# Moving the product of wide waves and growth from VectorE to GpSimd while a long kernel is made, and one semaphore for two groups of loads

## The reference, cut to what matters

```
dt = exp(log_dt); A = A_re + 1j*A_im; C = C_re + 1j*C_im
dtA = dt[:, None] * A
dC  = C * (exp(dtA) - 1.0) / A
powers = exp(dtA[:, :, None] * arange(L))          # L = 512
K = 2.0 * einsum('dn,dnl->dl', dC, powers).real    # 256 channels, 64 states
```

## Time and profile before

| | |
|---|---|
| median of 3 runs | 1396.36 us (1394.72 to 1397.79) |
| the profiled execution | 1397.99 us, of which its span is 1396.2 us |
| PE | 1192.2 us busy (85% of the span) |
| DVE | 928.4 us (66%) |
| ACT | 476.3 us (34%) |
| POOL | 343.1 us (25%) |
| granted TensorE clock, mean | 0.929 of full speed |

### The profile page before, as it was taken

One profiled execution on the slowest core, in us unless ns is written; L12 is line 12 of the kernel. 1 busy time (PEld: TensorE's weight loads), 2 busy tenths in 40 slices (PEclk: granted clock), 3 DMA queues, 4 the chain that ended last, 5 costly groups with the idle time before them and its releaser, 6 DMA issues. The chain is left out here.

```text
span 1396.2 us, 17324 instructions
## 1 busy us (share of the span) xinstructions
PE 1192.2 (85%) x5149; PEld 694.9 (50%) x5149; DVE 928.4 (66%) x3415; ACT 476.3 (34%) x824; POOL 343.1 (25%) x603
## 2 busy tenths in 40 slices
PE   4666858999899799899989979999687539999997
PEld 3423433455456354545546535554363426667664
DVE  6668898778768777877877787888974581111110
ACT  3543531053324415225332531432414423322221
POOL 4225220023022203302322220330203222323332
PEclk9688978999899999999999999999897759999999
DMA  9102000200300300030030031021000135433321
GB/s 285 36 16 62 19 1 25 52 19 16 92 19 1 100 26 1 16 93 19 6 103 19 1 72 51 1 62 39 1 0 0 63 111 175 137 94 91 95 39 19
DMA packets 45351, 72.51 MB, mean 52 GB/s; under 512 B 8549, under 2 KB 27208, under 8 KB 45130
## 3 DMA queue, kind: packets, MB, share of 16 engines
q1 hardware_dynamic: 39114, 62.88, 15.4%
q0 software_dynamic: 6144, 8.52, 3.5%
HBM read 58.27 MB, written 13.07 MB: 51 GB/s over the span
## 5 line engine op out<-in xcount | busy, mean ns | idle before, releaser
L849 POOL TENSOR_SCALAR ve<-mv 128x2 f32<-128x2 f32 x74 | 17.1, 230 | 501.5 <-DVE mv L1120 501.4
L1703 PE MATMUL ps<-x,keys 128*128 128x512 f32 x256 | 128.3, 627 | 0.9 <-DVE hT L1214 0.6
L1878 PE MATMUL ps<-hT,values 128*128 128x512 f32 x256 | 119.8, 594 | 0.0
L2334 PE MATMUL experts_ps<-experts_yT,experts_fc 128*128 128x512 f32 x256 | 111.9, 595 | 1.2 <-ACT experts_yT L2259 1.2
L2346 PE MATMUL experts_ps<-experts_fc,experts_hT 128*128 128x256 f32 x512 | 112.0, 379 | 0.8 <-ACT experts_hT L2271 0.8
L1703 PE MATMUL ps<-zT_second,w 128*128 128x512 f32 x224 | 104.5, 600 | 6.3 <-ACT big L1641 6.2
L2346 PEld LDWEIGHTS experts_ps<-experts_fc,experts_hT 128*128 128x128 f32 x512 | 96.6, 190 | 14.6 <-ACT experts_hT L2271 1.6
L2243 DVE SCALAR_TENSOR_TENSOR experts_o<-experts_ps,experts_wh,experts_b2w 128x256 f32<-128x256 f32 x32 | 15.5, 484 | 128.6 <-PE experts_ps L2346 128.6
L1703 PE MATMUL ps<-w,big 128*128 128x256 f32 x448 | 99.1, 380 | 0.8 <-ACT big L1641 0.8
L2271 ACT ACTIVATE experts_hT<-experts_ps,experts_b 128x512 f32<-128x512 f32 x64 | 44.0, 687 | 155.3 <-PE experts_ps L2334 155.3
L1703 PEld LDWEIGHTS ps<-w,big 128*128 128x128 f32 x448 | 84.1, 190 | 13.3 <-ACT big L1641 1.6
(11 more groups left out here) (445 smaller groups left out, 2369.4 us busy)
## 6 DMA issues: line engine op xcount, KB each, us to landing
gT<-expert_gates SPq DMA_DIRECT2D x32, 512.0 KB, 7.6
experts_fc<-in_fc1T SPq DMA_DIRECT2D x8, 1024.0 KB, 5.3
experts_fc<-in_fc2T SPq DMA_DIRECT2D x8, 1024.0 KB, 9.1
xT<-in_xT SPq DMA_DIRECT2D x8, 512.0 KB, 3.5
x<-in_x SPq DMA_DIRECT2D x8, 512.0 KB, 3.5
expert_table<-tb SPq DMA_DIRECT2D x7, 528.0 KB, 6.5
out_x<-x SPq DMA_DIRECT2D x7, 512.0 KB, 5.7
w<-in_W SPq DMA_DIRECT2D x2, 1024.0 KB, 9.3
```

The costliest lines, as they stand in the source:

```text
L849: nc.gpsimd.tensor_scalar(o, i, c, None, ALU.add).then_inc(*tick(*event))
L1703: last = nc.tensor.matmul(o, l, r_, start=start, stop=stop)
L1878: last = nc.tensor.matmul(bank("O2", k), S["values"][:, c, k * P:(k + 1) * P], hT[:, c % RING, :], start=(c == 0), stop=(c == HC - 1))
L2334: last = nc.tensor.matmul(g_bank(m), fc1[e % 3][:, k, m * P:(m + 1) * P], yT[e % 2][:, k, :], start=(k == 0), stop=(k == DC - 1))
```

## The change

POOL gets a stage `powers`: it waits for the pass's sines and exponentials and does the wide product, in place, with a signal of its own, `k_lift`. DVE's `powers` loses that product. PE's `powers` waits for both `k_pow` and `k_lift`, and POOL's `phases` from pass 2 on for `k_lift` of pass p-2 as well. As POOL now has a function named `powers`, SCHEDULE puts it, for each pass, where DVE's stands. The three small loads signal `w1_in`, and whoever waited for `w1_in` at 80 or for `row_in` at 48 now waits for `w1_in` at 128.

```diff
+    y.declare("waves_lifted", [("k_lift", p) for p in passes])
...
-            sp.dma_start(S["mgate"][:], A["mod_gate"].partition_broadcast(P)).then_inc(row_in, 16)
-            sp.dma_start(film_row_f[:, 0:2 * D], A["b_film_in"]).then_inc(row_in, 16)
-            sp.dma_start(film_row_f[:, 2 * D:4 * D], A["b_film_out"]).then_inc(row_in, 16)
+            sp.dma_start(S["mgate"][:], A["mod_gate"].partition_broadcast(P)).then_inc(w1_in, 16)
+            sp.dma_start(film_row_f[:, 0:2 * D], A["b_film_in"]).then_inc(w1_in, 16)
+            sp.dma_start(film_row_f[:, 2 * D:4 * D], A["b_film_out"]).then_inc(w1_in, 16)
...
                 if p >= 2:
                     g.wait_ge(*at(0, "k_pow", p - 2))
+                    g.wait_ge(*at(0, "k_lift", p - 2))
...
+            def powers(_, p):
+                k = p % 2
+                g.wait_ge(*at(0, "k_sin", p))
+                g.wait_ge(*at(0, "k_exp", p))
+                g.tensor_tensor(Us[k], Us[k], UEs[k], ALU.mult).then_inc(*tick("k_lift", p))
...
                 v.wait_ge(*at(0, "k_exp", p))
-                nc.vector.tensor_tensor(Us[k], Us[k], UEs[k], ALU.mult)
                 nc.vector.tensor_tensor(WAs[k], WAs[k], WEs[k], ALU.mult).then_inc(*tick("k_pow", p))
...
             def powers(_, p):
                 each = PC // QUARTERS
                 pe.wait_ge(*at(0, "k_pow", p))
+                pe.wait_ge(*at(0, "k_lift", p))
...
-                v.wait_ge(w1_in, 80)
+                v.wait_ge(w1_in, 128)
...
-                v.wait_ge(row_in, 48)
+                v.wait_ge(w1_in, 128)
...
-                        a.wait_ge(row_in, 48)
+                        a.wait_ge(w1_in, 128)
...
-                pe.wait_ge(w1_in, 80)
+                pe.wait_ge(w1_in, 128)
```

More of the change, by code:

```diff
@@ L601, in layers_block @@
             "par_in", "kv_in", "wq_in", "wo_in", "mask_in", "sel_in", "keys_in", "values_in"))
-        text_in, film_loaded, row_in, w1_in, dft_in, ffn_in, coef_in = (sem(n) for n in ("text_in", "film_loaded", "row_in", "w1_in", "dft_in", "ffn_in", "coef_in"))
+        text_in, film_loaded, w1_in, dft_in, ffn_in, coef_in = (sem(n) for n in ("text_in", "film_loaded", "w1_in", "dft_in", "ffn_in", "coef_in"))
         masks_made, film_folded, film_row_made, means_made, wq_centred = (sem(n) for n in (
@@ L952, in choose @@
                 g.memset(needed[:, 1:STEPS - 1, 4:7], 2.0 * CAP - N - 0.5).then_inc(tables_made, 1)
-            trips(g, {"choose": choose, "phases": phases, "fold_film": fold_film, "film_split": film_split_rows, "norm": norm_first, "attend": attend, "gates": gates, "rows": rows, "norm_ffn": norm_ffn, "ffn": ffn,
+            trips(g, {"choose": choose, "phases": phases, "powers": powers, "fold_film": fold_film, "film_split": film_split_rows, "norm": norm_first, "attend": attend, "gates": gates, "rows": rows, "norm_ffn": norm_ffn, "ffn": ffn,
                       "norm_out": norm_out, "scores": scores, "scales": scales})
```

## The result

The kernel after takes 1399.80 us, the median of 20 runs (1396.91 to 1402.53), the kernel before 1397.78 beside it (1393.41 to 1402.01). The ratio is 1.0025, with an interval of 1.0016 to 1.0034: slower by some 3.5 us (2.2 to 4.8). A ratio in this document is an estimate over all runs of both kernels, not the quotient of the two medians, which lie 2.0 us apart here (the means 3.4). The prediction said 1399.7, against the 1396.4 it started from: +3.3. That 1399.7 falls beside the median of 1399.80 is partly luck, as the kernel before now has 1397.78 and not 1396.4; the number to compare is the difference.

A forecast was written before the change was run, and what follows sets the result against it. VectorE, not TensorE, was taken to bound the first 195 us. Steps of 1.8 + 0.2 - 1.5 + 1.5 + 0.7 + 0.65 = 3.35, taken as +3.3 on the median 1396.4, gave 1399.7 us; range 1395.5 to 1404.

The forecast's parts named there:

- price of the lift: The wide product moved to GpSimd: 2.3 us alone, 2.2 in turn with VectorE, for VectorE's 1.23.
- pass 0: Sines and exponentials come 1.5 us earlier, but phases 1 end at 51.1 instead of 49.3: +1.8 us.
- pass 1: GpSimd's attention product stands behind the moved product, TensorE's transpose begins at 84.3 for 84.08: +0.2 us.
- pass 2 and fold_film: k_pow +0.85, but fold_film leaves the gates of batch 0, which end 1.5 us earlier: -1.5 us.
- passes 3 and 4: fold_film beside phases 5, film_split shifted beside powers 4, taps 4 at 148.85 instead of 146.84: +1.5 us.
- pass 5: Moved and narrow product need till 163.8 for 162.7, taps 163.8 for 163.09: +0.7 us.
- passes 6 and 7: Pass 6's narrow product ends 0.9 late; pass 7's moved product partly covered by a PSUM read: +0.65 us.
- The turns: VectorE instructions with two SBUF inputs and GpSimd's products run in turn, each 0.15 to 0.2 us shorter than alone.
- rival of the cheap lift: Moved product takes 1.91 us, or half of a pass's waits have slack: 3.2 less, 1396.5 us; chance 0.22.
- the one of VectorE untouched: The pair takes no turns, VectorE keeps its 1.23 us in passes 2, 5, 6, 7: 1391.5 us; chance 0.12.
- rival of the clock: TensorE returns 1.8 us later in pass 0, stays at 1.2 GHz longer: 3.5 us more, 1403; chance 0.14.
- the lock's rule: The skill's port pair held for whole instructions, without 0.15 overlap, would cost 2.4 us more; the prediction followed the rows.

The follow-up runs named there:

- fold_early: Kernel after with fold_film ahead of powers 3 in SCHEDULE, beside the gates of the first batch as before: 1397.56 us, ratio 1.0004.
- no_lift: Kernel after without the wide product, GpSimd's new stage keeping only its waits and signal: 1381.70 us, ratio 0.9886.
- lift_twice: Kernel after with the wide product done twice on GpSimd, first into a tile nobody reads: 1416.00 us, ratio 1.0141.
- split_lift: Kernel after with film_split directly behind film_row and fold_film behind powers 7: 1400.86 us, ratio 1.0022.
- loads_only: Kernel before with only the loads' part: three small loads signal w1_in, everyone waits for 128: 1396.09 us, ratio 0.9991.
- fold_late: Kernel before with fold_film moved in SCHEDULE to behind powers 7: 1395.62 us, ratio 0.9992.
- p1_first: Kernel after with GpSimd's phases 1 ahead of its moved product of pass 0, as before: 1398.97 us, ratio 1.0008.
- no_product: Kernel before with VectorE's wide product L1055 left out and no stage on GpSimd: 1387.22 us, ratio 0.9932.
- split_early: Kernel before with fold_film behind powers 7 and film_split directly behind film_row: 1393.95 us, ratio 0.9971.
- split_again: The kernel of split_early measured a second time, in the same rounds as split_lift: 1391.20 us, ratio 0.9966.

## Why the prediction was right, and where only in sum

By its own steps, in the profiled executions; "gain" is negative:

| step | predicted | measured |
|---|---|---|
| price of the lift | 2.3 alone, 2.2 in turn | 2.33, 2.20 |
| pass 0 | +1.8 | +3.1 at 56.7, then 0 at 64.4 (+2.0 at 55.6 in fold_early) |
| pass 1 | +0.2 | +0.2, and +1.0 by the clock |
| pass 2 and fold_film | -1.5 | -1.7 |
| passes 3 and 4 | +1.5 | +1.9 |
| pass 5 | +0.7 | +1.0 |
| passes 6 and 7 | +0.65 | +0.7 |
| taps 7 | +3.35 | +3.1 |
| loads | 0 | 0 |

**Right.** The turns, their size, and the price from the slope of two rows. The rival of the cheap lift (1.91) and the one of VectorE untouched fall with the 2.33 and with L1051's 3.36; the slack that the first also allowed falls with the 2.1 a pass of the second lift. So do the wide phases of pass 0 (1.23 at 28.18), the narrow product of pass 2 held (k_pow +0.88, forecast 0.85), the gates freed, and taps 4 at 148.2 (forecast 148.85), though there the narrow product came last and not the lift. From pass 2 on every step is within 0.4. Leaving the product out shows that the price is the product's: 12.3 us between none and one at taps 7 (11 without the earlier start of that execution).

**Pass 0: missed in this execution, met in others.** "So the sines and exponentials come 1.5 earlier" did not come true in the profiled execution. The phases did end at 31.4. But ScalarE has a copy of TensorE's result ahead of the sines; it came at 32.58 in this execution, where it came at 31.26 before:

```profile
32.58 1.01 ACT L1497 COPY keys<-ps 128x1024 f32<-128x1024 f32 x1 [1.79 <-PE ps L1763]
```

```profile
31.26 1.01 ACT L1490 COPY keys<-ps 128x1024 f32<-128x1024 f32 x1 [1.79 <-PE ps L1755]
```

The sines start at 33.61, 0.2 sooner, and phases 1 thus end 3.1 late and not 1.8. But three more kernels have the same order here (no_lift, lift_twice and fold_early), and in their profiles the copy comes at 31.3 to 31.5 and the sines at 32.36 to 32.54, 1.3 to 1.4 sooner than before, which is nearly the forecast (in split_lift, the fourth, at 33.32). In fold_early, whose work is that of the kernel after up to 100 us, the sines and the last of phases 1:

```profile
32.54 1.45 ACT L1470 ACTIVATE yv<-xf,sinA 64x512 f32<-64x512 f32 x2
...
50.59 0.69 DVE L1043 SCALAR_TENSOR_TENSOR xf<-tb,yv 128x512 f32<-128x512 f32 x1
```

Phases 1 end at 51.28 there (forecast 51.1) and TensorE's matmul behind the copy starts at 55.58, 2.0 after the kernel before (forecast 1.8). So the step was sized right, and 1.1 of the 3.1 are a scatter that has nothing to do with the change: the copies wait for eight matmuls on the keys, whose row took from 3.67 to 6.59 us in the twelve profiles. I had named this cover (the copies) and taken it as fixed; why it varies stays open.

**Right for the wrong reason at 64 us.** The rival of the clock was in the list with the opposite sign: a later return would hold TensorE at 1.2 GHz longer. In the profiled execution the later return met 2.4 GHz instead and paid back all 3.1 (the rival's 3.5 us had no row behind it; 6.83 less 3.71 is the price that the rows show). Then another stretch cost 1.0 (TensorE's matmuls from 86 us take 9.87 for 8.87; these are 88 to 92 us, after and then before; the clock's difference, 0.54 of 2 us in sum, is 1.08 us of work at 2.4 GHz):

```profile
88.00:90.00 2.00, 2.00 (x4) 0.91 (x3) 1.93 (x3) 0.00 (x0) 0.00 (x0) 0.50 0.00 0
90.00:92.00 2.00, 2.00 (x4) 0.78 (x3) 1.68 (x3) 0.21 (x1) 0.00 (x0) 0.61 0.00 0
```

```profile
88.00:90.00 2.00, 2.00 (x4) 0.74 (x4) 1.97 (x2) 0.00 (x0) 0.33 (x1) 0.65 0.00 0
90.00:92.00 2.00, 2.00 (x7) 0.80 (x6) 1.90 (x4) 0.58 (x1) 0.00 (x0) 1.00 0.00 0
```

The +2.0 forecast for passes 0 and 1 came out as +1.2, the sum of +3.1, -3.1, +0.2 and +1.0, which is no confirmation of it. How much of pass 0's loss is kept in an average run isn't settled. The times of before hint at how large that is: 7 of its 20 runs lie at 1393.4 to 1394.7, the others from 1396.4 on. The profiles with short bias matmuls (the kernel after 1396.91, loads_only 1393.45, fold_late 1393.98, fold_early 1395.47, lift_twice 1415.15) lie among the shorter runs of their kernels; those with 6.83 (before 1397.99, p1_first 1400.31, no_product 1390.86, split_early 1395.94, split_again 1395.71) among the longer. no_lift (1377.89, with 6.83) and split_lift (1403.09, with 3.73, the second longest of twelve) break the pattern. This is a fit, not a test.

**Wrong on the carry.** "A microsecond won or lost before shifts all that follows by as much, apart from TensorE's clock" fails by several us in most of the kernels. Against the kernel before, in us, taps 7 (one execution each) and time (from the ratio):

| kernel | taps 7 | time |
|---|---|---|
| no_lift | -9.1 | -15.9 |
| no_product | -7.7 | -9.5 |
| loads_only | -4.2 | -1.3 |
| fold_late | -3.1 | -1.1 |
| split_early, split_again | -1.6, -1.3 | -4.1, -4.8 |
| p1_first | +2.8 | +1.1 |
| after | +3.1 | +3.5 |
| fold_early | +5.0 | +0.6 |
| split_lift | +6.3 | +3.1 |
| lift_twice | +19.8 | +19.7 |

The signs agree throughout, but the two columns differ by up to 4.5, and by 6.8 for no_lift: the exception that I made for the clock is as large as the rule. So the 3.5 of the ratio agrees with 3.3, but within a scatter of several us that the price alone does not explain, and that the sum was met this closely is partly luck.

On the lock's rule: no holding for a whole instruction without overlap is seen. The lift ends 2.20 after its turn began, against 2.33 alone, and L1051 1.08 after it, against 1.22. The Trainium skill (SBUF — State Buffer, Who interferes with whom) says that the two engines' contention is an exclusive lock, and that the one who issued first blocks the other; the alternation agrees with it, to 0.15 us at each change of hands. The lost turns of the next but one section do not: there the instruction of VectorE had begun first and still came last.

## What to carry to other kernels

An engine whose work holds up that of the bound is a poor place to put the bound's work: here a turn of 2.2 us replaced 1.2, and it held also instructions of VectorE from which nothing had been moved. Price such a move as both engines in one queue, with the slow one's duration, and look at what stands around it in the slow engine's order, since it waits there too. Before believing a gain or loss of a few us, look at where TensorE's granted clock changes in both profiles, and measure by a landmark behind the edit rather than by the span.

## What was not expected of the hardware

**VectorE can lose its turn.** In most places VectorE's waiting instruction came next after one of GpSimd. Behind the cast of pass 4 (143.93 to 145.31) it did not: L1063, begun at 144.45, stood through the lift as well and took 3.71. It is not this one place alone. The kernel p1_first has the same 3.71 at 144.36. In lift_twice the same instruction stands through the cast and both lifts, so it loses its turn a second time, and behind a product:

```profile
151.05 6.00 DVE L1067 TENSOR_TENSOR xf<-xf,x 128x512 f32<-128x512 f32 x1
151.88 2.33 POOL L835 TENSOR_TENSOR vf<-big 128x1024 f32<-128x1024 f32 x1
154.18 2.33 POOL L836 TENSOR_TENSOR big<-big 128x1024 f32<-128x1024 f32 x1
```

In split_early (and split_again, 3.69) the first of phases 5, 1.22 alone, stands through two products with no cast between them, L822 (127.38 to 129.28) and L823:

```profile
127.70 3.68 DVE L1043 TENSOR_TENSOR big<-zT_second,it_i 128x1024 f32<-128x1024 f32 x1
129.25 1.04 POOL L823 TENSOR_TENSOR x<-zT_second,it_j 128x512 f32<-128x512 f32 x1
```

In split_lift L1063 beside a cast whose successor came 0.08 later (122.71 to 124.09, then 124.17) got in between and took 1.32. But elsewhere VectorE got its turn also where GpSimd's next instruction followed without a gap (L1051 at 40.45), so what decides it stays open.

**The same matmuls, 3.1 us apart.** The 32 bias matmuls took 6.83 in six profiles, at 1.2 GHz throughout (a granted clock of 0.50 in each), and 3.7 to 3.95 in six others, in kernels whose work before them differed by 1 to 3 us or, as between before (6.83) and fold_late (3.95), not at all.
